# Third layer's cross-attention: middle work of a slot in one piece, keys split by GpSimd, ScalarE's exponentials spread between the fill copies

## The reference

```python
ci = rms_norm(hidden_states, ln_post_cross_w)
cq = heads(ci @ cq_w, NH, CHD)
ckv = encoder_outputs @ ckv_w
ck, cv = jnp.split(ckv, 2, axis=-1)
ck, cv = (heads(ck, NH, CHD), heads(cv, NH, CHD))
cctx = sdpa(cq, ck, cv, causal=False)
hidden_states = hidden_states + cctx @ cdense_w
```

## Time and profile before

| | |
|---|---|
| median of 3 runs | 2375.14 us (2371.19 to 2375.70) |
| the profiled execution | 2373.76 us, span 2372.0 us |
| TensorE busy | 2309.4 us (97%) |
| VectorE busy | 1576.2 us (66%) |
| ScalarE busy | 1288.7 us (54%) |
| GpSimd busy | 668.8 us (28%) |
| the stage | about 1006 to 1506 us, 21% of the span |
| chain that ended last, by engine | PE 89%, ACT 5%, DVE 3%, DMA 2% |

### The profile page before, as it was taken

One profiled execution on the slowest core, in us unless ns is written; L12 is line 12 of the kernel. 1 busy time (PEld: TensorE's weight loads), 2 busy tenths in 40 slices (PEclk: granted clock), 3 DMA queues, 4 the chain that ended last, 5 costly groups with the idle time before them and its releaser, 6 DMA issues.

```text
span 2372.0 us, 42261 instructions
## 1 busy us (share of the span) xinstructions
PE 2309.4 (97%) x16486; PEld 1901.8 (80%) x16486; DVE 1576.2 (66%) x4256; ACT 1288.7 (54%) x2204; POOL 668.8 (28%) x752
## 2 busy tenths in 40 slices
PE   6989999999999999899999999999999999999999
PEld 4858999999999895466666666556899999999978
DVE  3357777777777656677777777414777777777764
ACT  2235555555555543267777777412655555555553
POOL 0045444444433224200000000011543434444330
PEclk9999999999999999989999999999999999999999
DMA  8720112121211110010000000310111111111010
GB/s 272 222 66 17 53 37 59 30 59 30 60 32 42 55 36 21 4 51 27 28 28 28 27 14 2 127 36 4 31 46 46 44 46 43 46 43 46 28 54 17
DMA packets 36137, 116.04 MB, mean 49 GB/s; under 512 B 4618, under 2 KB 18546, under 8 KB 35938
## 3 DMA queue, kind: packets, MB, share of 16 engines
q1 hardware_dynamic: 33474, 101.04, 14.0%
q10 hardware_dynamic: 2464, 12.29, 2.0%
HBM read 112.40 MB, written 0.92 MB: 48 GB/s over the span
## 4 chain that ended last, share of the span: by engine, by line
PE 89%; ACT 5%; DVE 3%; DMA 2%; POOL 0%; issue 0%; ACTq 0%; SPq 0%; DVEq 0%; POOLq 0%
PE bank L1061 20%; PE bank L1048 19%; PE bank L1075 12%; PE bank L1812 8%; PE bank L589 7%; PE bank L2078 3%; PE bank L1825 3%; PE bank L1798 3%; ACT n_scores L1927 2%; PE bank L1772 2%; PE bank L2091 2%; PE bank L688 2%; PE bank L885 1%; PE bank L1776 1%; PE bank L1242 1%; PE bank L1087 1%
## 5 line engine op out<-in xcount | busy, mean ns | idle before, releaser
L1111 ACT CAST p_T_high<-bank 125x512 fp32r<-125x512 f32 x672 | 350.7, 595 | 516.5 <-PE bank L1075 516.5
L1168 DVE TENSOR_TENSOR p_T_low<-bank,p_T_high 125x512 fp32r<-125x512 f32 x672 | 422.5, 684 | 257.9 <-ACT p_T_high L1111 257.9
L1134 DVE CUSTOM_DVE_ANT_0 scores<-bank,mask 128x500 f32<-128x500 f32 x672 | 418.4, 672 | 0.8 <-PE bank L1048 0.8
L1121 ACT ACTIVATE scores<-scores,row_max 128x1500 f32<-128x1500 f32 x224 | 353.4, 1578 | 2.7 <-DVE row_max L1139 2.7
L1061 PE MATMUL bank<-p_T_high,keys_nat_high 125*128 125x256 f32 (+1 forms) x1152 | 346.0, 300 | 1.7 <-ACT inverse L1118 1.7
L1061 PE MATMUL bank<-p_T_high,keys_nat_low 125*128 125x256 f32 (+1 forms) x1152 | 346.3, 301 | 0.0
L1061 PE MATMUL bank<-p_T_low,keys_nat_high 125*128 125x256 f32 (+1 forms) x1152 | 346.1, 300 | 0.0
L1075 PE MATMUL bank<-ident,scores 128*125 128x128 f32 x2688 | 331.1, 273 | 2.7 <-ACT scores L1121 2.7
L1075 PEld LDWEIGHTS bank<-ident,scores 128*125 128x125 f32 x2688 | 318.2, 187 | 5.7 <-ACT scores L1121 5.7
L1048 PE MATMUL bank<-keys_T_high,q_stage_high 128*128 128x500 f32 x672 | 280.1, 417 | 0.0
L1962 DVE CUSTOM_DVE_ANT_0 n_scores<-bank,n_zeros 112x500 f32<-112x500 f32 x384 | 236.9, 673 | 58.7 <-PE bank L1798 58.7
(11 more groups left out here) (244 smaller groups left out, 3624.0 us busy)
## 6 DMA issues: line engine op xcount, KB each, us to landing
ctx_T<-in_ctxT SPq DMA_DIRECT2D x32, 750.0 KB, 4.3
ctx_nat<-in_ctx SPq DMA_DIRECT2D x32, 672.0 KB
q_and_o<-in_ctxT SPq DMA_DIRECT2D x16, 750.0 KB, 9.0
n_ctx_T<-in_ctxT SPq DMA_DIRECT2D x16, 750.0 KB, 4.2
q_and_o<-in_ctx ACTq DMA_DIRECT2D x16, 672.0 KB
mask_bytes<-in_mask SPq DMA_DIRECT2D x32, 187.5 KB, 5.1
weights<-in_L_W SPq DMA_DIRECT2D x4, 1024.0 KB, 6.9
ctx_nat<-in_ctx SPq DMA_DIRECT2D x32, 78.0 KB
```

What stands on the lines that cost most here:

```text
L1111: e.copy(PTs[0][g % 2][0:KP, 4 * c:4 * c + 4, lo:lo + 128], psum[3 + c][0:KP, :].rearrange("p (k r) -> p k r", k=4)).then_inc(s_eh, 1)
L1121: e.activation(SB[s % 2], SB[s % 2], ACT.Exp, bias=mx[:, s % 4, 3:4], accum_out=mx[:, s % 4, 4:5]).then_inc(s_ex, 1)
L1134: e.tensor_tensor_reduce(out=SB[u % 2][:, c * CHK:(c + 1) * CHK], in0=psum[c][:, 0:CHK], in1=mb[:, c * CHK:(c + 1) * CHK], scale=1.0, scal ...
L1168: e.tensor_tensor(low, psum[3 + c][0:KP, :].rearrange("p (k r) -> p k r", k=4), high.bitcast(F32), ALU.subtract).then_inc(s_el, 1)
```

## The change

It edits nothing outside the narrow stage. `product` writes each product to two engines in turn: odd ones are copied out by ScalarE, even ones by VectorE, whole. For keys that is a plain fp32 copy into `CK`; GpSimd then makes the high part (a rounding copy) and the low part (a subtraction, in the place of the whole keys) and signals `s_n_cut`, for which the scores wait. `CK` lies where `CK_low` lies, so no memory is added. On TensorE both products, or all four key blocks of sums, stand in one piece between fills 0, 1 and fills 2, 3 of the slot. On ScalarE a slot's order becomes: with s % 3 of 1 or 2 that unit's exponential, two fill copies, with s % 3 = 0 the exponential of unit 0, the product copy, the third fill copy, and with s % 3 = 2 the exponential of unit 3. The statistics get three buffers. The reciprocal moves behind the maxima.

```diff
-        n_st = sbuf("n_stats", 2 * 4 * 5, scope=narrow).rearrange("p (a r x) -> p a r x", a=2, r=4)
+        n_st = sbuf("n_stats", 3 * 4 * 5, scope=narrow).rearrange("p (a r x) -> p a r x", a=3, r=4)
...
         def n_prod_out(b, i):
-            return (s_n_prod_act, 5 * b + (4 if i == 3 else 5)) if i in (3, 5) else (
-                s_n_prod_dve, 4 * b + min(i, 3) + 1)
+            return (s_n_prod_act, 3 * b + i // 2 + 1) if i % 2 else (s_n_prod_dve, 3 * b + i // 2 + 1)
+
+        def n_keys_cut(b, i):
+            return s_n_cut, 6 * b + 2 * i + 2
...
             def scores(s):
-                on.wait_ge(*n_prod_out(b, c))
+                on.wait_ge(*n_keys_cut(b, c))
...
-                for k in range(lo, lo + 2):
+                for k in range(lo, lo + 4):
...
-                    if made:
-                        product(*made[half])
-                    if b < B:
-                        sums(b, lo + 2 * half)
+                    if half == 0:
+                        for of in made:
+                            product(*of)
+                        if b < B:
+                            sums(b, lo)
...
+        def n_product_out(e, on, b, i):
+            at_bank = n_prod_bank(b, i)
             on.wait_ge(s_n_prod, 6 * b + i + 1)
             if i < 3:
+                if b >= 2:
+                    on.wait_ge(*n_scored(6 * (b - 1) - 1, 3))
+                dst, src = CK[b % 2][:, i * CHK:(i + 1) * CHK], at_bank[:, 0:CHK]
+            else:
+                if b >= 3:
+                    on.wait_ge(s_n_pv, b - 2)
+                dst = CV[b % 3][0:KP, 4 * (i - 3):4 * (i - 2), :]
+                src = at_bank[0:KP, :].rearrange("p (k c) -> p k c", k=4)
+            if i % 2:
                 e.copy(dst, src).then_inc(s_n_prod_act, 1)
+            else:
                 e.tensor_copy(dst, src).then_inc(s_n_prod_dve, 1)
...
             def exp(quad, r):
-                if quad >= 2:
-                    on.wait_ge(s_n_rc, quad - 1)
+                if quad >= 3:
+                    on.wait_ge(s_n_rc, quad - 2)
...
-                if 0 <= done < QUADS:
-                    exp(done, (0, 2, 3)[s % 3])
+                if 0 <= done < QUADS and s % 3:
+                    exp(done, s % 3)
                 if 0 <= quad < QUADS:
-                    for t in ts[0:3]:
+                    for t in ts[0:2]:
                         n_fill(e, on, quad, t)
                 if 0 <= done < QUADS and s % 3 == 0:
-                    exp(done, 1)
-                for b, i in n_products_of(s):
-                    act_product_out(e, on, b, i)
+                    exp(done, 0)
+                for b, i in n_products_of(s)[1:]:
+                    n_product_out(e, on, b, i)
+                if 0 <= quad < QUADS:
+                    n_fill(e, on, quad, ts[2])
+                if 0 <= done < QUADS and s % 3 == 2:
+                    exp(done, 3)
...
-                if s % 3 == 0 and 0 <= s // 3 - 2 < QUADS:
-                    recip(s // 3 - 2)
...
                 if s < SLOTS:
                     maxima(s)
+                if s % 3 == 0 and 0 <= s // 3 - 2 < QUADS:
+                    recip(s // 3 - 2)
...
         def pool_narrow(e, on):
+            def keys_cut(b, i):
+                at = slice(i * CHK, (i + 1) * CHK)
+                on.wait_ge(*n_prod_out(b, i))
+                if b >= 2:
+                    on.wait_ge(*n_scored(6 * (b - 1) - 1, 3))
+                e.tensor_copy(CK_high[b % 2][:, at], CK[b % 2][:, at]).then_inc(s_n_cut, 1)
+                on.wait_ge(s_n_cut, 6 * b + 2 * i + 1)
+                e.tensor_tensor(CK_low[b % 2][:, at], CK[b % 2][:, at], CK_high[b % 2][:, at].bitcast(F32),
+                                ALU.subtract).then_inc(s_n_cut, 1)
+
...
+                for i in range(3):
+                    keys_cut(b, i)
```

63 lines of the change are left out of this document (21 added, 42 removed).

## The result

The changed kernel takes 2357.2 us (median of 13 runs, 2348.1 to 2362.8) against 2375.1 (13 runs, 2365.8 to 2382.8): a ratio of 0.9912, with a 95% interval of 0.9899 to 0.9925. The forecast was 2358.3, between 2351 and 2369. The medians differ by 17.9 us; the ratio stands for 20.9 us, and its interval for 17.8 to 24.0. The profiled execution took 2350.4.

A forecast was written before the change was run, and what follows sets the result against it. Bound by TensorE's order, plus holes in j=4 and j=1 from ScalarE's order. -0.76 us a batch over 14.0 batches (-10.6), drain -0.7, start -5.5: -16.8, so a median of 2358.3 us; range 2352 to 2362, with rivals (a)-(c) 2351 to 2369.

The forecast's parts named there:

- holes, ScalarE's order: TensorE's waits for late fill copies in j=4 and j=1 (j: slot's place in its batch, 0-5) go: 0.71 us a batch.
- turns between kinds: TensorE's middle work in one piece saves 0.40 us a batch in sums slots, 0.06 in products slots, together 0.46.
- new wait for exponential 3: In j=3 the slot's second fill waits for exponential 3, last in ScalarE's preceding slot: 0.41 us a batch lost.
- batch: Six slots of the stage: the three terms together -0.76 us, from 29.66 to 28.90.
- start, once: Slot 4's wait for a fill copy shrinks from 1.60 to some 0.5 us, the clock stays full: 5.5 us saved.
- drain, once: The drain behind the window has two sums slots: counted as -0.7 us.
- cost 0: GpSimd's split of the keys, 6 us a batch on a nearly idle engine, delays nothing; at the start at most 2 us.
- (a): Rival: the clock falls at the start all the same; price 5.0 us, 2363 us; chance 0.16.
- (b): Rival: the hole moves, exponential 3 costing in j=0 and j=3 what j=4 lost; nothing gained at start; 2368 us; chance 0.10.
- (c): Rival: TensorE's one piece saves nothing, 32 sums cost 1.79 us and fills to scores over 1.05; 2365 us; chance 0.06.
- (d): Rival: slower; the copy of t6 is 0.8 us late in j=2 and j=5, delaying exponential 3; 2388 us; chance 0.06.
- (e): Rival: VectorE's output product waits for a GpSimd subtraction of 1.26 us; 13 us in all, 2372 us; chance 0.01.

The follow-up runs named there:

- e10: e6 with TensorE's middle work (products, sums) in halves again and the product's copy last in ScalarE's list: 2354.5 us, ratio to the kernel before 0.9917.
- e6: Changed kernel with the exponential of unit 3 moved ahead of the product's copy and the third fill copy: 2345.5 us, ratio to the kernel before 0.9867.
- e5: Changed kernel with the keys' split given back to ScalarE (high part) and VectorE (low part): 2356.2 us, ratio to the kernel before 0.9917.
- e9: Changed kernel with two statistics buffers again and the reciprocal back ahead of the maxima: 2352.6 us, ratio to the kernel before 0.9898.
- e7: Changed kernel with the old order of ScalarE's exponentials in the first quad alone: 2362.4 us, ratio to the kernel before 0.9949.
- e2: Kernel before with TensorE's middle work (products, sums) in one piece and nothing else: 2390.9 us, ratio to the kernel before 1.0076.
- e8: Changed kernel with four more GpSimd subtractions ahead of each split of the keys: 2360.4 us, ratio to the kernel before 0.9926.
- e3: Changed kernel with ScalarE's exponentials in the order of the kernel before: 2374.9 us, ratio to the kernel before 0.9997.
- e1: Changed kernel without the one piece, TensorE's products and sums again in two halves: 2386.6 us, ratio to the kernel before 1.0044.
- e12: e6 with additions for GpSimd at the time of the output's last product on VectorE: 2346.3 us, ratio to the kernel before 0.9884.

## Why the prediction was right

It was right in the time and in its mechanism, but two gains of the sum were too small, one of them by much, and so was the loss. With e10 and e6 each can be told apart: before less e10 is what the holes in j=4, 1 and 3 cost, e10 less e6 what the turns cost together with the wait in j=2 that e10 shares with before, after less e6 what the new wait costs (us a batch; e10 and before differ also in the keys' split and the buffers, which e5 and e9 show at nothing in after).

| term | forecast | measured |
|---|---|---|
| holes, ScalarE's order | -0.71 | -1.16: j=4 -0.58, j=1 -0.31, j=2 -0.18, j=3 -0.08 |
| turns between kinds | -0.46 | -0.53: sums slots -0.51, products slots -0.02 |
| new wait for exponential 3 | +0.41 | +0.59: j=3 +0.54, j=0 +0.05 |
| batch | -0.76 | -1.10 |
| start, once | -5.5 | -5.9 |
| drain, once | -0.7 | -0.5 |

**TensorE's pieces.** The 32 sums take 1.65 to the next fill (1222.53 to 1224.18), as read from the earlier trace rows. The sums slots gave 0.51 instead of 0.40, since in j=4 the last fill block meets transposes. The products slots gave 0.02 where 0.06 was taken, and nothing near the bound of 0.4.

**The holes.** j=4's was read right, 0.57 against 0.58. The rest is where the sum fell short: 0.14 was taken for j=1 and nothing for j=2 and j=3, and it is 0.57. j=1's was an estimate of a quarter of the other, "as there only one fill copy is late and by less", and is 0.31; the earlier trace rows show the exponential and the fill block behind it, and j=1's own pieces could have been added up as j=4's were. j=2's 0.18 was overlooked: the product's copy at the end of ScalarE's list makes exponential 2 late there, and with it the copy of t4. j=3's 0.08 is what before has above e10; what makes it was not taken apart.

**The new wait.** Place and size are right: in j=3, and hardly in j=0. The 0.13 between 0.41 and 0.54 are three small terms: the exponential starts 0.15 after the scores instead of 0.10 (the product's copy stands ahead of the third fill copy), TensorE goes on 1.70 after that start instead of 1.66, and the restart takes 0.09 instead of 0.05. That the fill would go at 1.40 unhindered is what e6 shows. What the wait hangs on is the place of exponential 3 behind the third fill copy, while ScalarE stands idle for 1.1 us ahead of the product's copy; e6 puts it there and gains the 0.59.

**The start.** The mechanism stands: the clock stayed full, and the slots 4 to 6 take 3.8, 3.3 and 3.7 us, 3.6 in the mean against "rather 3.5". The wait in slot 4 is 0.25 us, where "some 0.5" was taken. e7 puts the gain on the order in the first quad, and e2 shows that a wait shortened to 1.24 us keeps the full clock as well.

**GpSimd.** 87 us of work were added, "some 90"; e8 shows that three times the work changes no batch. VectorE's maxima in j=1 start 1.91 us into the slot and end at 4.37, as worked out (1.99 and 4.4). Cuts 0 and 1 cost nothing at the start, where slots 0 to 3 together take 14.2 us in both kernels; e8 shows what they would cost if they came late. e5 agrees with "cost 0" for the split, and e9 for the buffers and the reciprocal. But the argument that VectorE and ScalarE "lose instructions" and nothing more is incomplete: with the old order the split is worth up to 1.48 a batch (e2 against e3, which also have the buffers between them), with the order of e6 0.25, with after's 0.

**The rivals.** (a) did not come: with the wait at 0.25 us the clock held, and both e3 and e7 show it falling when the long wait returns. (b) came in part: 0.59 of the 1.16 came back as the new wait. (c) falls by e10. (d) is what e1 and e2 show, in other kernels: a copy that is late in an engine's list costs more than the pieces save. Here the copy of t6 was not late by 0.8, but by about 0.05. (e) did not come, for the reason given against it: GpSimd's cuts fall in j=2 and 3 and the product in j=1. That the two would exclude each other is right, as the rows beside e12 show; had they met, the price would have been real.

**The sum.** The 21.0 us between first and last scores are the start's 5.9 and some 13.7 batches of 1.10 us. In the profiled executions the stage with its drain thus became 21.5 us shorter, where 16.8 was forecast: short by 0.34 a batch, 4.7 us, and most of that by the holes. The ratio's interval stands for 17.8 to 24.0, and the forecast gain of 16.8 lies below it. That the median came within 1.1 us of the number is luck of the scatter: by the traces and by the ratio the change gives some 4 to 5 us more than was forecast.

## What to carry to other kernels

Ask of each instruction in an in-order list what stands behind it, and look in the same list for idle time that an urgent instruction could fill: the best edit here was one exponential moved by two places, into a gap of 1.1 us. Judge an edit together with the lists of the other engines: the piece alone made the kernel 0.8% slower, the rest of the change without the piece 0.4% slower, and the piece with a new order of ScalarE's list, and nothing else, 1.0% faster. To price something with no waits in it, build the kernel that has none and change that one thing; the price read from a kernel full of waits is a sum. And look for the waits in the rows of the weight loads too: the kernel that was built here to have none (e10) had one in every batch, a quarter of the difference, and the matmuls' rows did not name it.

## What the runs showed that was not expected

One late copy in one slot at the start costs 6 to 7 us (e3, e7), far more than its own 1.6 us, as the granted clock then stands at 1.2 GHz for some 14 to 17 us. It fell behind single waits of TensorE of 1.60 (before), 1.64 and 1.73 (e3), 1.67 (e7) and 1.75 us (e2), and during one of 5.27 us (e8). It stayed at 1.00 behind one of 1.24 us (e2), and from 1060 to 1475 with waits of 0.3 to 0.8 us, one a batch or more (after and e1). In the first slots of the stage all kernels have a short low stretch besides (0.66 from 1015 to 1020 before, 0.74 in after), which takes nothing from the comparison.

What a turn between kinds of matmuls costs depends on the pair: fills and sums in turn cost 0.13 us a slot more than in one piece, while fills and products in turn, of keys (j=1) or of values (j=3), cost 0.01.

A VectorE instruction with two inputs in SBUF that starts while a GpSimd instruction of that kind is under way ends at a fixed distance behind that one's end: 0.41 us for 128x384 (1.50 us in all instead of 0.56), 0.07 for 128x56 (254 ns in the median instead of 217). From the length alone the second looks like a small surcharge; that its end follows the other's end shows the wait.
